# A transformer layer with a routed expert stage on one core: how rows are sorted for their experts and how results find their way back

## The reference, cut to what matters

```python
x1 = _layernorm(x + attn_out, g1, be1)
gate_logits = x1 @ Wg + bg                     # [4, 1024, 8]
topk_p, topk_i = jax.lax.top_k(softmax(gate_logits), 2)
topk_p = topk_p / jnp.sum(topk_p, axis=-1, keepdims=True)
comb = jnp.sum(one_hot(topk_i, E) * topk_p[..., None], axis=-2)
h = gelu(x1 @ W1[e] + b1[e])                   # every expert e: 128 -> 512
y = h @ W2[e] + b2[e]                          # 512 -> 128
moe_out = sum over e of comb[e] * y[e]
return _layernorm(x1 + moe_out, g2, be2)
```

## Time and profile before

| | |
|---|---|
| median of 3 runs | 1771.5 us (1768.04 to 1774.88) |
| profiled execution | 1773.69 us, span 1771.5 us |
| PE busy | 1462.7 us (83%) |
| DVE busy | 1267.5 us (72%) |
| ACT busy | 1169.6 us (66%) |
| POOL busy | 378.3 us (21%) |
| chain that ended last | PE 19%, DVE 18%, DMA 12% |

### The profile page before, as it was taken

The page is one execution under the profiler, slowest core; times in us unless marked ns, Lnnn a source line. Parts: engine busy times, 40 slices in busy tenths (PEclk is TensorE's granted clock), DMA queues, the critical chain, the costliest instruction groups (busy, mean ns, idle before and its releaser), DMA issues.

```text
span 1771.5 us, 39180 instructions
## 1 busy us (share of the span) xinstructions
PE 1462.7 (83%) x15249; PEld 671.4 (38%) x15249; DVE 1267.5 (72%) x1972; ACT 1169.6 (66%) x2373; POOL 378.3 (21%) x418
## 2 busy tenths in 40 slices
PE   5679999989998788559999998999889978964980
PEld 2324444444444455212222222222222236853970
DVE  6787777778785266599999998999899842510254
ACT  7537677777687655318999997899779964421341
POOL 5300000000000355200000002000213321656364
PEclk9869899999899999759999999999999989986995
DMA  4513422121112343400000020002001314552773
GB/s 137 191 55 116 143 80 93 41 81 61 62 41 70 89 122 117 148 22 27 36 32 36 35 69 32 31 33 69 31 33 50 110 36 136 177 167 81 231 223 108
DMA packets 132777, 152.94 MB, mean 86 GB/s; under 512 B 13744, under 2 KB 107824, under 8 KB 132336
## 3 DMA queue, kind: packets, MB, share of 16 engines
q1 hardware_dynamic: 122480, 123.43, 22.4%
q0 software_dynamic: 10112, 27.01, 4.1%
HBM read 90.90 MB, written 63.46 MB: 87 GB/s over the span
## 4 chain that ended last, share of the span: by engine, by line
PE 19%; DVE 18%; DMA 12%; issue 7%; ACT 4%; another core or an unknown queue 2%; POOL 2%; SPq 1%; ACTq 0%; POOLq 0%; DVEq 0%
DVE row_max L629 14%; DMA sorted_in<-v_all,slots 8%; PE bank L596 6%; PE banks L572 4%; PE banks L540 2%; PE banks L1434 2%; ACT probs L683 2%; PE banks L1444 2%; DMA qk_parts<-parts 1%; DMA expert<-expert_rows 1%; POOL pair_out L1234 1%; DVE probs L1801 1%; DMA probs<-x_mid_d 1%; DMA pair_out<-k_work,pairs 1%
## 5 line engine op out<-in xcount | busy, mean ns | idle before, releaser
L629 DVE TENSOR_REDUCE row_max<-banks 128x2 f32<-128x1024 f32 (+3 forms) x896 | 938.9, 1104 | 137.7 <-PE banks L546 74.5
L683 ACT ACTIVATE probs<-banks 128x512 f32<-128x512 f32 (+3 forms) x1792 | 879.7, 551 | 191.7 <-PE banks L572 90.9
L596 PE MATMUL bank<-probs,v_ones 128*32 128x256 f32 (+3 forms) x7168 | 536.6, 377 | 20.0 <-ACT o_sums L694 16.8
L540 PE MATMUL banks<-k_work,q_work 48*128 48x512 bf16 (+3 forms) x1792 | 366.7, 382 | 75.2 <-DVE row_max L629 59.3
L572 PE MATMUL banks<-q_work,k_work 51*128 51x512 bf16 (+3 forms) x1792 | 385.3, 373 | 51.0 <-DMA q_work<-max_T 33.3
L572 PEld LDWEIGHTS banks<-q_work,k_work 51*128 51x128 bf16 x1792 | 102.3, 93 | 420.2 <-ACT probs L683 318.6
L721 POOL DMA_DIRECT2D heads_out<-o_sums x64 | 35.6, 556 | 1011.6 <-ACT o_sums L694 1011.6
L596 PEld LDWEIGHTS bank<-probs,v_ones 128*32 128x32 f32 x7168 | 147.3, 109 | 255.9 <-ACT probs L683 184.6
L2041 ACT ACTIVATE rope<-banks,expert 128x256 f32<-128x256 f32 x184 | 71.8, 473 | 156.5 <-PE banks L1434 107.0
L540 PEld LDWEIGHTS banks<-k_work,q_work 48*128 48x128 bf16 x1792 | 94.9, 96 | 141.6 <-DVE row_max L629 107.9
L1444 PE MATMUL banks<-expert,rope 128*128 128x128 f32 x736 | 96.6, 288 | 28.7 <-DVE v_ones L1745 17.6
(11 more groups left out here) (209 smaller groups left out, 1165.2 us busy)
## 6 DMA issues: line engine op xcount, KB each, us to landing
expert<-expert_rows SPq DMA_DIRECT2D x46, 578.0 KB
qk_parts<-parts SPq DMA_DIRECT2D x64, 256.0 KB, 3.4
heads_out<-o_sums POOLq DMA_DIRECT2D x64, 256.0 KB, 4.4
q_work<-qk_parts SPq DMA_DIRECT2D x64, 128.0 KB
k_work<-qk_parts SPq DMA_DIRECT2D x64, 128.0 KB
sorted_in<-zeros SPq DMA_DIRECT2D x4, 1472.0 KB, 13.1
parts<-sorted_in SPq DMA_DIRECT2D x22, 256.0 KB
q_work<-qk_parts SPq DMA_DIRECT2D x64, 64.0 KB
```

The costliest lines, as they stand in the source:

```text
L540: last = pe.matmul(to[:, par, 0:width], q[r:r + M0, pair, qt * P:(qt + 1) * P], k[r:r + M0, pair, kh * G:kh * G + width], start=True, stop ...
L596: last = pe.matmul(bank[7][32 * j:32 * j + 32, c0 + part * w:c0 + (part + 1) * w], v_ones[i % QB][:, kt, j, :], prob_slots[:, (e + j) % RI ...
L629: dve.tensor_reduce(row_max[:, qt, 2 * pair:2 * pair + 2, kh], self.buf_of("chunk", g, c)[:, :, 0:width], AX.X, ALU.max).then_inc(s["chunk ...
L683: act.activation(prob_slots[:, e % RING, 0:width], banks46[:, e % EXP_BANKS, 0:width], ACT.Exp, scale=SCALE).then_inc(s["exps"], 1)
```

## The change

- A row in `sorted_in` has 129 numbers (516 bytes). The last one is the row number of its result in `pair_out`; rows that nobody writes keep 1.0e6 from a fill. `name_rows` writes the numbers beside `x1` for choice 0, and again for choice 1 once the scatters of choice 0 have landed. `keep_rows` copies them to `pairs` when a block's rows are there. `give_out` skips rows with a number out of bounds. The inverse (`spot_ids`, `make_spots`, `make_places`, `make_marks`, `invert`, `make_pairs`) is gone.
- Every expert has a region of its own in `sorted_in`, so a row's slot no longer depends on the block counts. The DRAM tensors are larger. They are filled by 34 DMAs in the groups 1 to 12 of the first attention, before by 4 DMAs in its groups 0 to 3.
- Batch 2 is sorted and scattered alone (stage 1, 16 scatters) as soon as the last attention group is done. Batch 3 (stage 2, 16 scatters) goes behind it in each region.
- The rows of a block are loaded at an address read into a register (`block_row`), one load for a block, with 5 buffers. (`ROWS_FROM` is block 20, `RANKS_FIRST` is 1.) `load_ahead` issues four experts and four row loads.

```diff
-X_RUN, X_BUFS = 2 * SIDES, 3
+X_BUFS = 5
-ON_WAY = (1, 2)
-GIVEN_FIRST = 6
+ON_WAY = (1, 2, 2)
+GIVEN_FIRST = 4
+STAGE_TILES = ((0, ST), (0, TILES), (TILES, ST))
...
+            def load_rows(m):
+                section, j = divmod(m, BLOCKS)
+                sp.wait_ge(end["blocks"], section + 1)
+                if j == 0:
+                    wait_lanes(sp, scatter_number(section * (STAGES - 1), TOPK * (TILES if section else ST) - 1))
+                if m >= X_BUFS:
+                    sp.wait_ge(end["xsT"], m - X_BUFS + 1)
+                which = sp.value_load(block_row[0:1, section, j:j + 1], min_val=0, max_val=REGION - 1)
+                rows = xs_d[section].rearrange("(n k p) d -> n p k d", k=SIDES, p=P)
...
                     sp.wait_ge(rows_made, 16 * len(made))
-                    for m in range(W_BUFS - 1):
+                    for m in range(W_BUFS):
                         load_expert(m)
-                    for i in range(2):
-                        load_rows(0, i)
+                    for m in range(X_BUFS - 1):
+                        load_rows(m)
...
+                        if j == ROWS_FROM:
+                            load_rows(BLOCKS)
+                        if j >= ROWS_FROM:
+                            load_rows(BLOCKS + 1 + j - ROWS_FROM)
...
+            def name_rows(stage, i):
+                a, b = STAGE_TILES[stage]
+                at = (TILES * JOINED if stage else 0) + a
+                if i == 0:
+                    pool.wait_ge(end["slots"], stage + 1)
+                    pool.wait_ge(end["x1"], HALVES * (at + b - a) // TILES)
...
+                else:
+                    wait_lanes(pool, scatter_number(stage, b - a - 1))
+                pool.tensor_tensor(x1_rows[:, at:at + b - a, D], token_f[:, at:at + b - a], shift[:, i, 0:b - a],
+                                   ALU.add).then_inc(end["named"], 1)
+                pool.wait_ge(end["named"], TOPK * stage + i + 1)
...
             def give_out(m):
-                section, j = divmod(m, BLOCKS)
-                if j == 0:
-                    pool.wait_ge(end["pairs"], section + 1)
                 pool.wait_ge(end["y"], m + 1)
                 for side in range(SIDES):
...
+                    pool.indirect_dma_start(pair_d, bass.IndirectOffsetOnAxis(pairs[:, m, side:side + 1], 0),
+                                            y_of(m)[:, side, :], None, bounds_check=TOPK * T - 1, oob_is_err=False
+                                            ).then_inc(lane_out[n % LANES], 16)
...
             attend[2].pool(pool, fronts)
-            for j in range(2):
-                give_out(j)
+            name_rows(1, 0)
+            scatter(1, 0, 0, TILES)
             for k in range(HALVES):
                 end_root(B - 1, k)
-            for j in range(2, GIVEN_FIRST):
+            name_rows(1, 1)
+            scatter(1, 1, 0, TILES)
+            for j in range(GIVEN_FIRST):
                 give_out(j)
             shares(1)
-            scatter(1, 0, ST)
+            for i in range(TOPK):
+                name_rows(2, i)
+                scatter(2, i, 0, TILES)
             for j in range(GIVEN_FIRST, BLOCKS):
                 give_out(j)
...
             pe.wait_ge(end["gate"], HALVES * FIRST)
-            invert(0)
...
                     up(m)
+                    if m == RANKS_FIRST:
+                        ranks(1)
...
+                link(dve.tensor_tensor(slot_te[:, a:b, :], within, base[:, :, :].broadcast_to([P, n, E]), ALU.add))
+                for i in range(TOPK):
+                    last = dve.tensor_tensor(slot_pick[:, i, a:b, :], chosen[:, i, a:b, :], slot_te[:, a:b, :], ALU.mult)
+                link(last)
+                link(dve.tensor_reduce(slots_f[:, :, a:b], slot_pick[:, :, a:b, :], AX.X, ALU.add))
...
             def keep_rows(m):
                 dve.wait_ge(end["xs_T"], m + 1)
                 if m >= 2:
                     dve.wait_ge(end["up"], m - 1)
+                dve.tensor_copy(pairs[:, m, :], xs_in[:, m % X_BUFS, :, D])
                 dve.tensor_copy(xsT[:, m % 2, :], bank[X_BANK][:, 0:SIDES * P]).then_inc(end["xsT"], 1)
...
                         if m == 0:
                             keep_rows(0)
-                            make_pairs(0)
+                            best(JOINED)
+                        if m == RANKS_FIRST:
+                            sort(1)
                         if m + 1 < SECTIONS * BLOCKS:
                             keep_rows(m + 1)
                     if m == 0:
+                        choose(1)
                         attend[2].reciprocals(dve, B - 1)
```

More of the change, by code:

```diff
@@ L529, in free @@
                     else:
-                        pe.wait_ge(end["sort"], 5)
+                        pe.wait_ge(end["slots"], 1)
                 def chunk(g, c):
@@ L750, in build @@
         end = {x: sem(f"end_{x}") for x in FRONT}
-        end.update({x: sem(f"end_{x}") for x in ("gate", "gap", "e2", "picked", "ranks", "sort", "slots", "blocks", "marks", "inverse", "pairs", "counted",
+        end.update({x: sem(f"end_{x}") for x in ("gate", "gap", "e2", "picked", "ranks", "slots", "blocks", "counted",
                                                  "xs_T", "xsT", "up", "gelu", "down", "y",
                                                  "sum", "link", "tail_moments",
-                                                 "tail_offset", "normal", "scaled", "weighted")})
+                                                 "tail_offset", "normal", "scaled", "weighted", "named")})
         end_heads = [sem(f"end_heads_here{i}") for i in range(HALVES)]
@@ L763, in build, with scatter_number, given_number, x1_of @@
         LOAD_FROM = GROUPS - QB
-        def scatter_number(section, i):
-            return (TOPK * ST + GIVEN_FIRST * SIDES) * section + i
-        def given_number(section, at):
-            return (TOPK * ST if section == 0 and at < GIVEN_FIRST * SIDES else 2 * TOPK * ST) + PLACES * section + at
+        SCATTER_FROM = (0, TOPK * ST, TOPK * (ST + TILES) + GIVEN_FIRST * SIDES)
+        def scatter_number(stage, i):
+            return SCATTER_FROM[stage] + i
+        def given_number(m, side):
+            return TOPK * (ST + TILES) + SIDES * m + side + (0 if m < GIVEN_FIRST else TOPK * TILES)
+        def x1_of(q, first, last):
+            return x1_rows[:, q * TILES + first:q * TILES + last, 0:D]
         def wait_lanes(eng, n):
@@ L879, in build @@
             made.append((expert_d[e, :, 2 * FF + FC:ROW], t["eb2"][e:e + 1, :].broadcast_to([P, D])))
+        fills = []
+        for i in range(SECTIONS):
+            rows = xs_d[i].rearrange("(p r) d -> p r d", p=P)
+            fills += [rows[:, r:min(r + FILL_RUN, FILL_ROWS), :] for r in range(0, FILL_ROWS, FILL_RUN)]
+        FILLS = -(-len(fills) // (NG - 4))
         LATE_RUN, MADE_RUN = -(-len(late) // (NG - 2)), -(-len(made) // (NG - 2))
@@ new lines, in scatter @@
+            def scatter(stage, i, first, last):
+                a, b = STAGE_TILES[stage]
+                section = 1 if stage else 0
+                for tile in range(a + first, a + last):
+                    n = scatter_number(stage, (b - a) * i + tile - a)
+                    landed(n - ON_WAY[stage])
+                    pool.indirect_dma_start(xs_d[section], bass.IndirectOffsetOnAxis(slots[:, section, i, tile:tile + 1], 0),
+                                            x1_rows[:, ST * section + tile, :], None).then_inc(lane_out[n % LANES], 16)
@@ L1375, in end_heads_product @@
                 pe.wait_ge(end["heads"], n + 1)
+                if q == B - 1:
+                    pe.wait_ge(end["slots"], STAGES - 1)
                 for g in range(GT):
@@ L1481, in _ @@
                         if j == RANKS_AT:
-                            ranks(section + 1)
+                            ranks(STAGES - 1)
             down(SECTIONS * BLOCKS - 1)
@@ new lines, in sort @@
+            def sort(stage):
+                a, b = STAGE_TILES[stage]
+                n = b - a
+                section = 1 if stage else 0
+                dve.wait_ge(end["ranks"], stage + 1)
+                within = rank_bank(stage)[:, 0:n * E].rearrange("p (t e) -> p t e", e=E)
+                total = rank_bank(stage)[:, n * E:(n + 1) * E]
+                base = region_on if stage == STAGES - 1 else region
+                link(dve.tensor_tensor(slot_te[:, a:b, :], within, base[:, :, :].broadcast_to([P, n, E]), ALU.add))
+                for i in range(TOPK):
+                    last = dve.tensor_tensor(slot_pick[:, i, a:b, :], chosen[:, i, a:b, :], slot_te[:, a:b, :], ALU.mult)
+                link(last)
+                link(dve.tensor_reduce(slots_f[:, :, a:b], slot_pick[:, :, a:b, :], AX.X, ALU.add))
+                if stage == STAGES - 1:
+                    link(dve.tensor_tensor(total_of[:, :, 0], total, total_of[:, :, 0], ALU.add))
+                else:
+                    link(dve.tensor_copy(total_of[:, :, 0], total))
```

(6 more changed lines are left out.)

317 lines of the change are left out of this document (117 added, 200 removed).

## The result

The changed kernel takes 1777.5 us in the median of 20 runs (1768.23 to 1786.6), the kernel before 1770.12 us beside it (1766.1 to 1775.81). The ratio is 1.0036, with a 95% interval of 1.0021 to 1.0052, so the change made the kernel a little slower here. Forecast were 1726 us. The profiled execution took 1783.7 us, with a span of 1781.9 us.

A forecast was written before the change was run, and what follows sets the result against it. POOL's string of scatters and `give_out` DMAs was taken to bound the expert stage: last `give_out` at 1689.4 with shifts, plus 34.65 us to the end, gave 1724, set at 1726 us as bounds lean upwards; range 1705 to 1766.

The forecast's parts named there:

- section 1's rows are there some 6 us after 1569; then 23 x 3.73 = 86 us: PE in the expert stage: section 1's 23 blocks at 3.73 us each, plus a few us for experts, ending at 1666.
- POOL bounds it: End of the expert stage: PE some 15 us ahead of POOL, so POOL's string sets the end.
- point 3: Expert stage before: PE's signals came late while POOL gave out 34 DMAs back to back until 1631.61, reason unknown.
- rival A: PE's signals late again as 38 plus 46 `give_out` run back to back at section 1's start: 1744 us, chance 0.24.
- shifts in: Times with the delays before the expert stage added: +4.2 us for row loads, +2.7 for section 0's scatters and DVE.
- first scatter of stage 1: POOL's start on batch 2: slots there at about 1480.5, name and scatters from 1481 before shifts, about 1488 with them.
- stage 2 done: POOL's second scatter stage: 16 scatters of 2.0 us plus 4 us for a landing, until 1569 before shifts.
- 84 `give_out` DMAs with four roots: End of POOL's string: 38 `give_out` in 48 us, then 46 with four `tail_root` of 1.9, 58 + 7.6, to 1682.5.
- B's mechanism: Rival B: the bounds check makes each `give_out` dearer on POOL; 1794 us at a spacing of 2.0 us, chance 0.12.
- what the last attention group loses: Before the last attention group: +4.2 us from four row loads, +2.7 with section 0's scatters; PE's wait about 12, not 7.65.
- The wait at the section's change: PE's wait for section 1's first rows: 5 to 8 us instead of 16.93.
- 516-byte rows: Section 0's scatters with rows grown from 512 bytes: 2 us taken, bounds 0 and 10.

The follow-up runs named there:

- held: Jobs in which the unchanged kernel before took 1774.9, 1773.07 and 1775.68 us, and 1770.12 beside the result; a level holds for the whole job.
- free: Jobs (1 and 3) in which the unchanged kernel before took 1742.97 and 1742.53 us; a level holds for the whole job.
- d_after: The changed kernel, no edit, run again in a free job: 1741.66 us, ratio 0.9996 to the kernel before.
- k4b: Changed kernel with the four expert row loads issued on SP behind the last attention group's maxima, second run, free job: 1732.0 us, ratio 0.9938.
- c_after: The changed kernel, no edit, run again in a held job: 1778.4 us, ratio 1.0031 to the kernel before.
- k1: Changed kernel with a waited-for 128x512 POOL fill behind each of section 0's 38 late `give_out` DMAs, free job: 1776.27 us, ratio 1.0198.
- k10: Changed kernel with maxima ahead of row loads and a 128x1 POOL fill behind each block's second late section 0 `give_out`, held: 1750.6 us, 0.9861.
- k2: Changed kernel with section 0's 38 late `give_out` DMAs each waiting until the one before landed, free job: 1822.33 us, ratio 1.0449.
- k7: Changed kernel with maxima ahead of row loads and third and fourth batch scatters four on their way, not two, held: 1770.81 us, ratio 0.9977.

## Why the prediction was wrong, step by step

**The step that failed** is this sum's "section 1's rows are there some 6 us after 1569; then 23 x 3.73 = 86 us", with no stall in it, and "POOL bounds it" on top. It priced a PE that works through the burst, against a reference of 1771.5 us in which PE lost 32 us to the same kind of stall. I had seen the stall (point 3, "I do not know why") and given it to rival A with 0.24. But the change leaves the burst as dense as it was, and it moves PE no faster out of it. In all six traces of the two kernels from held jobs it is there, and in the one from a free job it isn't. By my estimate for the kernel before, the gain forecast was thus mostly the difference between two kinds of jobs: 1771.5 against 1739.5.

**Held: where the time went.** The end of attention is 15.4 us later (its last value matmul 1471.5 before, 1486.9 after). The 15 us less at the change of section pay for that: PE reaches it at 1593.33 before and 1594.30 after. Then PE gets three blocks through the burst before and one after. Two blocks are 7.5 us. The last `give_out` moves by 9.8 us and the end by 10.4; the medians differ by 7.4, as this execution is 6.2 us over its median and that of before 3.6. So what PE would have won, it would have spent waiting in the burst: the stall ends some 4 to 6 us behind POOL's burst, at 1636 to 1640 in both.

**Rival A was right in kind and too cheap.** It let POOL catch up at 1618 + 7, and PE have 20 blocks left and end 3 us ahead of POOL. It was 1634 to 1640, 22 blocks, and some 10 us ahead, as POOL stands before `tail_root` for 20.60 us and then has a backlog. 15 + 7.5 + 7 us on 1744 give 1774. Of the 8 us that are left to the span of 1781.9, 7.4 are short waits of PE between 1694 and 1733.

**Free: the forecast's mechanism.** There it can be held against d_after step by step.

| step | forecast (shifts in) | d_after |
|---|---|---|
| first scatter of stage 1 | 1488 | 1489.52 |
| stage 1 done | 1527 | 1528.2 |
| `shares` done | 1540 | 1541.7 |
| stage 2 done | 1576 | 1576.8 |
| last `give_out` | 1689.4 | 1702.98 |
| from there to the end | 34.65 | 35.0 |
| end | 1724 | 1738.0 |

POOL's string is the bound, PE's last matmuls start at 1689.42, ahead of it. But PE was put at 1666 + 7 = 1673 for the end of its blocks, and is 18 us later; it waits 11.0 us for ACT in the expert stage, 5.7 at most. So it is not some 15 us ahead of POOL, as forecast, but 11.5. In POOL's string one term is off: 84 `give_out` DMAs with four roots were put at 113.4 us and took 125.9. The bounds check costs 0.03 us each (1.29 in place of 1.26), 2.5 us in all, so B's mechanism is small. The other 10 us are waits of up to 2.4 us, mostly for landings, in a string that I had taken as gapless. k4b, 9.7 us less for a string that starts 10 us sooner, agrees. But there the kernel before takes 1742.5 too, and nothing is won: I forecast 1771.5 - 45, and by the estimate above the stall made up 32 of the 45.

**Right, in part by luck:** what the last attention group loses. Forecast were +6.9 us, and it is +7.5. The wait was put at about 12, which leaves out the 2.7 us of the scatters that my own sum has before it; it is 15.11. And the parts are off both ways, the loads (5.2 us forecast) too high and the scatters too low: the last scatter 46.75 us behind the group's maxima in place of 43.30 (+3.4), the first row load 3.57 us behind it in place of 2.32 (+1.3), and 3.9 us for four loads in place of 1.0 (+2.9). The other 8 us of attention: about 2 recur in the three traces of the changed kernel (48.7 to 49.1 us from the maxima of the group before section 0 is sorted to the next, 46.1 to 46.7 in the four of before). The rest comes and goes: 5.6 us stand at the end of the first attention already (565.44 for its row of maxima, 559.88 before), and c_after, with the same fills, has it at 561.26, k1 at 560.57. The wait at the section's change was forecast at 5 to 8 us and is 1.94. 516-byte rows: with two scatters on their way nothing is to be seen (in stage 2 of d_after they follow at 2.02 and 2.15 us, before at 2.0). With one on its way, in section 0, the shortest step from one to the next is 2.54 us in the three traces of the changed kernel and 2.48 or 2.49 in the four of before, and the median 2.59 to 2.74 in place of 2.52. My 2.5 us was thus the median; with longer waits now and then the mean is 3.07 to 3.09 before and 3.17 to 3.26 after. No run separates the longer rows from the new layout of `sorted_in`. By the Trainium skill ("DMA: Bandwidth & Descriptors", "How a descriptor splits into AXI transactions") a row that doesn't start at a 256-byte boundary costs an extra partial transaction. The 0.05 us between the shortest steps are within the tenth of a us that I estimated from it, and don't single it out.

**Open:** why PE is held up in some jobs and not in others, and by what path; why the dense `give_out` DMAs of section 1 mostly don't do it; and the kernel before in a trace of a free job.

## What to carry to other kernels

A long wait that no semaphore explains ("remote", "issue" with no cause) must be explained or priced in both branches before a gain is booked behind it: ask whether the change removes its cause, and if it doesn't, subtract nothing. Where POOL issues indirect DMAs back to back beside another engine's work, try a short pause after every second one; it took the stall away here, but cost over 1% where there was none. And measure in more than one job, since a burst can be free in one and cost 30 us in the next. A load that waits for late data belongs behind every transfer on its queue that doesn't.

## What the runs showed of the hardware

- Back to back indirect DMAs on POOL (1.26 to 1.29 us apart) stop or slow PE in some jobs (the held ones), for up to 27 us at a time, and its signals reach DVE and ACT 30 and 40 us late. A fill of 0.14 us with its wait, after every second one, is enough to end that where it stands (k10, 20.00 of 20 us of PE in both stretches).
- PE then runs at the lower of its two clock levels (1.2 GHz): the granted clock is 0.58 and 0.59 in the two stretches of the stall and 1.00 in the same stretches of d_after, and a group of 16 matmuls takes 3.54 us there and 1.95 at 1588.68, ahead of the stall.
- An indirect DMA with bounds check costs POOL 1.29 us where one without costs 1.26.
- The distance between indirect DMAs depends on how many may be on their way: 3.4 us in the mean with one (k2; 2.5 us in the median of section 0's scatters), 2.0 to 2.5 with two, 1.26 with four (k7).
